# Attention scores from 16-bit parts of queries and keys, in a two-layer attention and FFN kernel

## The reference, cut to what matters

```python
q = (layernorm(x) @ Wq.T + bq)      # per head: [64, 8]
k = (ctx @ Wk.T + bk)
v = (ctx @ Wv.T + bv)
p = softmax(q @ k.T * sqrt(8))      # per sequence and head, [64, 64]
x = x + concat_heads(p @ v) @ Wp.T + bp
```

## Time and profile before

| | us |
|---|---|
| median of 3 runs (1026.54 to 1030.34) | 1029.37 |
| the profiled execution | 1027.88 |
| span of its profile | 1026.1 |
| PE busy | 872.3 (85%) |
| DVE busy | 775.2 (76%) |
| ACT busy | 581.3 (57%) |
| POOL busy | 567.8 (55%) |

### The profile page before, as it was taken

How to read it: one execution, slowest core, us unless ns; L and a number is a source line. 1 busy time by engine, 2 the same in 40 slices (tenths; PEclk the granted TensorE clock), 3 DMA queues, 4 the chain that set the end, 5 groups by cost and what they waited for, 6 DMA issues and landing times. The chain is left out here.

```text
span 1026.1 us, 25789 instructions
## 1 busy us (share of the span) xinstructions
PE 872.3 (85%) x9415; PEld 623.1 (61%) x9415; DVE 775.2 (76%) x2300; ACT 581.3 (57%) x940; POOL 567.8 (55%) x642
## 2 busy tenths in 40 slices
PE   6837999855878775999999537999999999979997
PEld 1215777633555444666666425888888888846665
DVE  6786999878878672988888555788898876547774
ACT  2464888543444342666667523576767656347774
POOL 4400476568777773555555476665656551027775
PEclk9967999889999997999999856999999999989999
DMA  8744555233223244444444221232424240023442
GB/s 252 257 145 114 158 169 152 80 126 112 73 73 83 73 134 126 120 156 158 153 151 153 79 78 33 70 90 89 136 79 124 62 116 12 23 84 81 131 117 52
DMA packets 86909, 114.74 MB, mean 112 GB/s; under 512 B 36384, under 2 KB 55520, under 8 KB 86016
## 3 DMA queue, kind: packets, MB, share of 16 engines
q1 hardware_dynamic: 75856, 94.99, 31.2%
q0 software_dynamic: 8192, 16.79, 5.6%
q10 hardware_dynamic: 2736, 1.31, 0.5%
HBM read 73.73 MB, written 35.13 MB: 106 GB/s over the span
## 5 line engine op out<-in xcount | busy, mean ns | idle before, releaser
L1128 POOL TENSOR_TENSOR moe_h_lo<-moe_hid,moe_h_hi 128x512 f16<-128x512 f32 x78 | 90.3, 1159 | 92.2 <-ACT moe_h_hi L1285 87.6
L1833 ACT ACTIVATE split_table<-attn_psT 128x1024 f32<-128x1024 f32 x64 | 65.3, 1021 | 95.1 <-PE attn_psT L1711 88.1
L1391 DVE SCALAR_TENSOR_TENSOR moe_hid<-moe_psU,split_to_hidden,moe_act_g 128x512 f32<-128x512 f32 x110 | 80.5, 745 | 24.2 <-ACT moe_act_g L1279 24.0
L1279 ACT ACTIVATE moe_act_g<-moe_psG,split_unscale 128x512 f32<-128x512 f32 x110 | 75.8, 689 | 40.5 <-PE moe_psU L1210 36.6
L1285 ACT ACTIVATE moe_h_hi<-moe_hid 128x512 f16<-128x512 f32 x110 | 68.6, 624 | 32.8 <-DVE moe_hid L1391 32.8
L1900 DVE TENSOR_REDUCE split_table<-attn_psN 128x16 f32<-128x1024 f32 x62 | 75.2, 1214 | 12.1 <-PE attn_psN L1686 12.0
L1122 POOL DMA_INDIRECT scratch_xs<-cell_xn,res_row x64 | 63.0, 985 | 25.6 <-issue 19.1
L1628 POOL DMA_INDIRECT cell_h<-scratch_ys,res_slot x64 | 62.7, 980 | 19.7 <-issue 19.7
L1122 POOL DMA_INDIRECT scratch_xs<-moe_xn,res_row x64 | 62.1, 970 | 19.5 <-issue 19.5
L1628 POOL DMA_INDIRECT cell_y<-scratch_ys,res_slot x64 | 62.5, 977 | 17.8 <-issue 17.4
L1723 PE MATMUL attn_psO<-heads_vheads,split_table 128*64 128x18 f32 x2048 | 71.4, 212 | 0.1
(11 more groups left out here) (353 smaller groups left out, 2776.9 us busy)
## 6 DMA issues: line engine op xcount, KB each, us to landing
early_ctxT<-in_keys SPq DMA_DIRECT2D x16, 512.0 KB, 3.6
scratch_ys<-cell_h SPq DMA_DIRECT2D x26, 256.0 KB, 2.0
early_ctxT<-in_values SPq DMA_DIRECT2D x8, 544.0 KB, 3.8
mlstm_vals<-in_values SPq DMA_DIRECT2D x8, 544.0 KB, 3.8
scratch_fw<-ffn_table SPq DMA_DIRECT2D x8, 544.0 KB, 4.7
res_x<-in_x SPq DMA_DIRECT2D x16, 256.0 KB, 6.1
early_ctxT<-in_ctxT SPq DMA_DIRECT2D x16, 256.0 KB, 6.1
attn_in_ctxT<-attn_in_ctxT SPq DMA_DIRECT2D x64, 64.0 KB
```

The costliest lines, as they stand in the source:

```text
L1128: pool.tensor_tensor(h_lo[u % 3][c][:, :], hid[u % 2][c][:, :], h_hi[u % 3][c][:, :], ALU.subtract).then_inc(lo_done[c], 1)
L1279: act.activation(act_g[c][:, :], psG[c][:, :], ACT.Silu, scale=sw.unscale[:, 0:1]).then_inc(silu_done, 1)
L1391: v.scalar_tensor_tensor(out=hid[u % 2][c][:, :], in0=psU[c][:, :], scalar=sw.to_hidden[:, 0:1], in1=act_g[c][:, :], op0=ALU.mult, op1=ALU ...
L1833: act.activation(probT[i % 2][:, :, :, :, :].rearrange("p r b m q -> p (r b m q)"), psT[:, :], ACT.Exp).then_inc(prob_done, 1)
```

## The change

In the experts' stage a new class `ScoreOperands` prepares the keys. `k_out` now adds the key bias. VectorE takes the largest absolute key of every group; in slot tiles 5 to 8 the three engines form from it, and from the query weights, two scales, and scale the query weights and bias in place. From slot tile 10 on ScalarE scales each group's keys and writes their f16 high part, GpSimd the f16 low part, and SP stores both in a scratch tensor `kh`; 32 such halves are spread over 29 slot tiles. In the attention phase the three key buffers are cleared once, and SP loads each group's keys into them by eight transfers of 16 rows each, which leaves the other places zero: this takes the place of `k_out`'s masks. To make that possible the columns of the query and key weights are permuted on the host.

The queries are written as a high part by ScalarE (`q_hi`), then VectorE computes the low part and writes both parts twice, with masks (`split_q`). The score products become three f16 products each: high times high, high times low, low times high. The scale is taken back in the exponential. From group 3 on the normalised rows are written by ScalarE (`normalise_more`) with a factor and a start value that GpSimd forms (`begin`). `q_(g+2)` moves ahead of `values(g, 0)` on TensorE, `hb.clear` moves behind the first normalise on VectorE.

```diff
+    def half(self, act, n, raw, pairs):
+        g = n // 2
+        keys, pair = raw[:, g * GROUP:(g + 1) * GROUP], pairs[g % 2]
+        if n % 2 == 0:
+            act.wait_ge(self.ready, ONE + 1)
+            act.activation(keys, keys, ACT.Copy, scale=self.all[:, 0:1]).then_inc(self.scaled, 1)
+        else:
+            act.wait_ge(self.scaled, ONE + g + 1)
+            if g >= 2:
+                act.wait_ge(self.kept, ONE + 16 * (g - 1))
+            act.activation(pair[:, 0, :], keys, ACT.Copy).then_inc(self.high_done, 1)
+    def low(self, pool, g, raw, pairs):
+        pair = pairs[g % 2]
+        pool.wait_ge(self.high_done, ONE + g + 1)
+        pool.tensor_tensor(pair[:, 1, :], raw[:, g * GROUP:(g + 1) * GROUP], pair[:, 0, :], ALU.subtract).then_inc(self.low_done, 1)
...
+            def load_keys(g):
+                if g >= 3:
+                    sp.wait_ge(scores_done, ONE + 4 * (g - 2))
+                else:
+                    sp.wait_ge(cleared, ONE + g + 1)
+                for rr in range(HR):
+                    for m in range(HM):
+                        rows = slice((rr * HM + m) * ROWS, (rr * HM + m + 1) * ROWS)
+                        sp.dma_start(keys[g % 3][rows, :, :, m, :].rearrange("p w b t -> p (w b) t"),
+                                     s["kh"][g, rows].rearrange("p w (b t) -> p (w b) t", b=GB)).then_inc(keys_in[g % 3], 16)
...
             for g in range(GROUPS):
+                if there(g + 3):
+                    load_keys(g + 3)
                 store(g)
...
+            def begin(g):
+                k = g % 2
+                pool.wait_ge(ln.var_done, ONE + g + 1)
...
+                pool.tensor_scalar(minus[k][:, :], ln.mv[k][:, :, 0], -1.0, None, ALU.mult).then_inc(minus_done, 1)
+                ln.root(pool, g, k)
...
+                pool.tensor_tensor(start[k][:, :], minus[k][:, :], ln.rstd[k][:, :], ALU.mult).then_inc(start_done, 1)
...
                 for b2 in range(2):
                     b = 2 * i + b2
-                    for rr in range(HR):
-                        rows = slice(rr * RH, (rr + 1) * RH)
-                        ins = pe.matmul(bank[:, rr * 512 + b2 * HM * S:rr * 512 + (b2 + 1) * HM * S],
-                                        queries[g % 3][rows, b, :, :].rearrange("p n t -> p (n t)"),
-                                        keys[g % 3][rows, b, :, :].rearrange("p m t -> p (m t)"), start=True, stop=True)
+                    for n, (wq_, wk_) in enumerate(((0, 0), (0, 1), (1, 0))):
+                        for rr in range(HR):
+                            rows = slice(rr * RH, (rr + 1) * RH)
+                            ins = pe.matmul(bank[:, rr * 512 + b2 * HM * S:rr * 512 + (b2 + 1) * HM * S],
+                                            queries[g % 3][rows, wq_, b, :, :].rearrange("p n t -> p (n t)"),
+                                            keys[g % 3][rows, wk_, b, :, :].rearrange("p m t -> p (m t)"),
+                                            start=(n == 0), stop=(n == 2))
...
+            def normalise_more(g):
+                act.wait_ge(x_turned, ONE + g)
+                act.wait_ge(start_done, ONE + g + 1 - ON_V)
+                for t in range(TILES):
+                    ins = act.activation(xn[:, t, :], res.x[:, g * TILES + t, :], ACT.Identity, bias=start[g % 2][:, t:t + 1],
+                                         scale=ln.rstd[g % 2][:, t:t + 1])
+                ins.then_inc(xn_more, 1)
...
+            def split_q(g):
+                pair = both[g % 2]
+                v.wait_ge(q_hi_done, ONE + g + 1)
+                v.scalar_tensor_tensor(out=pair[:, 1, :], in0=psF[:, :], scalar=bq[:, 0:1], in1=pair[:, 0, :],
+                                       op0=ALU.add, op1=ALU.subtract).then_inc(q_lo_done, 1)
+                v.wait_ge(q_lo_done, ONE + g + 1)
+                if g >= 3:
+                    v.wait_ge(scores_done, ONE + 4 * (g - 2))
+                for n in range(HN):
+                    ins = v.tensor_scalar(queries[g % 3][:, :, :, n, :].rearrange("p w b t -> p (w b) t"),
+                                          pair.rearrange("p w (b t) -> p (w b) t", b=GB), qmask[:, n:n + 1], None, ALU.mult)
+                ins.then_inc(q_done, 1)
...
                 if one:
                     peak_of(g + 1, 2)
+                if two:
+                    split_q(g + 2)
                 if now:
                     heads_out(g, 0)
...
-                if three:
-                    normalise(g + 3)
```

More of the change, by code:

```diff
@@ L303, in keep, with halves_at, keys_split_at, __init__ @@
         sp.dma_start(s["fw"][e], table[:, :]).then_inc(self.table_out, 16)
+K_TOP = 32768.0
+SPLIT_FROM = 10
+HALVES = 2 * GROUPS
+def halves_at(j):
+    if j < SPLIT_FROM:
+        return range(0)
+    n = SLOT_TILES - SPLIT_FROM
+    return range((j - SPLIT_FROM) * HALVES // n, (j - SPLIT_FROM + 1) * HALVES // n)
+def keys_split_at(j):
+    return [n // 2 for n in halves_at(j) if n % 2]
+class ScoreOperands:
+    def __init__(self, nc, ctx, sems, sw, given):
+        r = self.room = Room(nc, ctx, sems, "operands")
+        self.given, self.ident, self.ones = given, sw.ident, sw.ones
+        self.tops, self.wide, self.top = r.sb("tops", [P, GROUPS]), r.sb("wide", [P, 2]), r.sb("top", [P, 2])
+        self.one, self.scales, self.all = r.sb("one", [1, 2]), r.sb("scales", [1, 4]), r.sb("all", [P, 4])
+        self.unscore = r.sb("unscore", [P, 1])
+        self.read, self.step, self.fed, self.ready = r.sem("read"), r.sem("step"), r.sem("fed"), r.sem("ready")
+        self.scaled, self.high_done, self.low_done, self.kept = r.sem("scaled"), r.sem("high"), r.sem("low"), r.sem("kept")
+    def largest_key(self, v, g, raw, k_raw):
+        v.wait_ge(k_raw, ONE + g + 1)
+        v.tensor_reduce(self.tops[:, g:g + 1], raw[:, g * GROUP:(g + 1) * GROUP], AX.X, ALU.max,
+                        apply_absolute_value=True).then_inc(self.read, 1)
+    def largest(self, v):
+        step, given = Steps(v, self.step), self.given
+        v.wait_ge(given.loaded, ONE + 16 * given.count)
+        v.wait_ge(self.read, ONE + GROUPS)
+        v.tensor_reduce(self.top[:, 0:1], self.tops[:, :], AX.X, ALU.max)
+        v.tensor_reduce(self.wide[:, 0:1], given.wq[:, :], AX.X, ALU.max, apply_absolute_value=True)
+        step(v.tensor_reduce(self.wide[:, 1:2], given.bq[:, :], AX.X, ALU.max, apply_absolute_value=True))
+        step(v.tensor_reduce(self.top[:, 1:2], self.wide[:, :], AX.X, ALU.max))
+    def invert(self, v, ps):
+        step = Steps(v, self.step)
+        step.at(2)
+        v.wait_ge(self.fed, ONE + 1)
+        step(v.tensor_reduce(self.one[:, :], ps[0:1, 0:2 * P].rearrange("o (n p) -> o n p", n=2), AX.X, ALU.max))
+        step(v.tensor_scalar(self.scales[:, 2:4], self.one[:, :], TINY, 1.0 / K_TOP, ALU.max, ALU.mult))
+        step(v.reciprocal(self.scales[:, 0:2], self.scales[:, 2:4]))
+    def apply(self, v, ps):
+        step, given = Steps(v, self.step), self.given
+        step.at(5)
+        v.wait_ge(self.fed, ONE + 2)
+        step(v.tensor_copy(self.all[:, :], ps[:, 0:4]))
+        for t in (given.wq, given.bq):
+            v.tensor_scalar(t[:, :], t[:, :], self.all[:, 1:2], 0.5 / D, ALU.mult, ALU.mult)
+        v.scalar_tensor_tensor(out=self.unscore[:, :], in0=self.all[:, 2:3], scalar=2.0 * D * SCALE1, in1=self.all[:, 3:4],
+                               op0=ALU.mult, op1=ALU.mult).then_inc(self.ready, 1)
+    def turn_largest(self, pe, ps):
+        pe.wait_ge(self.step, ONE + 2)
+        for n in range(2):
+            ins = pe.matmul(ps[0:1, n * P:(n + 1) * P], self.top[:, n:n + 1], self.ident[:, :], start=True, stop=True)
+        ins.then_inc(self.fed, 1)
+    def spread(self, pe, ps):
+        pe.wait_ge(self.step, ONE + 5)
+        pe.matmul(ps[:, 0:4], self.ones[:, :], self.scales[:, :], start=True, stop=True).then_inc(self.fed, 1)
+    def half(self, act, n, raw, pairs):
[13 more added lines that the diff above has]
+        pool.tensor_tensor(pair[:, 1, :], raw[:, g * GROUP:(g + 1) * GROUP], pair[:, 0, :], ALU.subtract).then_inc(self.low_done, 1)
+    def keep(self, sp, s, g, pairs):
+        sp.wait_ge(self.low_done, ONE + g + 1)
+        if g:
+            sp.wait_ge(self.kept, ONE + 16 * g)
+        sp.dma_start(s["kh"][g], pairs[g % 2][:, :, :]).then_inc(self.kept, 16)
@@ L1006, in phase_moe @@
         xnT = [r.sb(f"xnT{k}", [D, GROUP]) for k in range(2)]
+        pairs = [xnT[k][:, :].bitcast(F16).rearrange("p (w t) -> p w t", w=2) for k in range(2)]
         x_hi = [r.sb(f"x_hi{k}", [D, GROUP], F16) for k in range(2)]
@@ L1111, in _ @@
                     fw.feed(sp, a, j // 2, piece)
+                if j + 1 < SLOT_TILES:
+                    for g in keys_split_at(j + 1):
+                        ops.keep(sp, s, g, pairs)
             for b in range(3):
                 sp.wait_ge(y_out[b], ONE + 16 * len(range(b, SLOT_TILES, 3)))
+            sp.wait_ge(ops.kept, ONE + 16 * GROUPS)
         @block.gpsimd
@@ L1140, in _ @@
```

(12 more changed lines are left out.)

159 lines of the change are left out of this document (95 added, 64 removed).

## The result

The changed kernel takes 1051.93 us (median, 1050.82 to 1054.44) against 1029.86 for the kernel before in the same comparison: a ratio of 1.022, interval 1.019 to 1.025. It is slower by 22 us, where 10 us less was forecast, with a range of 1002 to 1033. The profiled execution took 1051.22 us, its span is 1049.4, 23.3 more than before.

What follows compares the result with a forecast made beforehand. TensorE looked to bound the kernel; after the change the table loop would bind groups 2 to 8. Experts +0.5, start -0.7, table loop +4.7, end -14.5 sum to -10.0 us: forecast 1018, range 1002 to 1033.

Steps and rivals of the forecast that it cites:

- TensorE's term: Attention groups: scores steps fall from 1.37 to 0.89 us, plain from 0.97 to 0.66, saving 3.2 us of 17.53.
- VectorE's new work: Per attention group: split_q comes at 1.65 us (bounds 1.5 and 3.2), normalise's 2.96 goes, 1.3 us less work.
- the gather loop's landing: Attention gathers: 2.48 us from the fourth gather's start to VectorE's combine, one part of the gather loop.
- the prediction's own sum: Gather loop through GpSimd and VectorE: 15.5 us a group, or 16.9 with low, both under 17.53.
- the two small ops: GpSimd, between statistics and the last four gathers: two added ops, estimated at 0.45 us.
- SP's keys: Eight key transfers a group, 5 us of issue, behind the table's store and ahead of need: cost nothing.
- The table loop: Attention groups 2 to 8: the weight table's trip through memory becomes the bound, 18.2 against 17.53 us, +4.7 in all.
- The last seven intervals: End of attention: three intervals become 15.5 us each (-5.7), four follow TensorE (-8.8), together -14.5 us.
- The start: Start of attention: gathers already set the pace, so splitting earlier keys gains little, -0.7 us (+2 to -4).
- The experts' stage: Preparing keys on ScalarE, GpSimd and VectorE, partly in the router's stage, costs +0.5 us (0 to +4).
- The clock: Attention groups 2 to 8: TensorE, idle some 3 us a group, at times runs two steps at lower clock, +0.4.
- Rival (c): Slower: table loop lengthens to 20.5 us with split_q at 3.2 and half-clock steps; +12.5, 1040 us; chance 0.13.

Runs made afterwards that it cites:

- e1: Changed kernel with all eight gathers of group g+4 on GpSimd ahead of begin(g+3), not four before and four behind: 1025.33 us, ratio 0.996.
- e3: Changed kernel with the weight table's store and the raw weight load cut to 64 columns each in groups 1 to 8: 1036.7 us.
- e2: Changed kernel with each key load from group 3 on moving 2 of its 16 rows, same number of transfers: 1040.89 us.
- e10: Changed kernel with the cuts of e2 and e3 together, few key rows and small weight transfers: 1040.46 us.
- e8: Kernel before the change, with its gathers in e1's order and nothing else: 1024.38 us, ratio 0.994.
- e5: e1 with scores(g,3) put ahead of plain(g+2,0) on TensorE: 1020.95 us.
- e6: e1 with the weight table stored in two halves, the high half ahead of x3's store, and high waiting only for that half: 1020.89 us.
- e7: e1, e5 and e6 together, with the starting raw weight loads behind group 2's gathers and group 1's keys behind the second combine: 1008.8 us, ratio 0.979.
- e11: Changed kernel with VectorE's largest key taken over 16 of the 512 columns of each group: 1048.56 us.
- e12: e7 with three exchanges: shift before out_ and peak(g+2,0), plain(1+g,1) behind scores(g,0), values copied ahead of the fourth exponential: 1002.1 us, ratio 0.971.
- e4: Changed kernel with normalise back on VectorE for all groups and begin reduced to the square root: 1046.78 us.

## Why the prediction was wrong

**TensorE's term was nearly right.** Plain was forecast at 0.66 and is 0.66, scores at 0.89 and is 0.99: 2.8 us a group saved instead of 3.2. The missing 0.1 is the end of the step: from the last block's start to the values' matmuls 0.32 us pass (752.53 to 752.85), where the next block follows after 0.23. The first three of e1's intervals behind the store of group 8 are 14.66, 14.66 and 14.65, close to the 14.3 given for TensorE alone.

**VectorE's new work was right.** split_q 1.65 forecast, 1.57 measured; each f16 pass takes 469 to 562 ns in all 32, so no hold as long as the 2110 ns of the earlier trace rows came to them. GpSimd ran no arithmetic beside any of them, so the Trainium skill's rule on the shared port (SBUF — State Buffer, section Who interferes with whom) is not tested by this trace.

**The step that failed is the gather loop's landing.** The text took "a gather started at 634.92 let VectorE combine at 637.40, 2.48", from the start of the stage, where SP had no transfer under way, and carried it into groups 2 to 8. There the landing is 5.6. The rest of that sum stands: statistics to the fourth gather is 6.57 (6.19 forecast), and 16.9 + 0.38 + 3.15 = 20.4. e1 shows the place (the gathers out of the loop: -2.4 a group), e3 and e2 the reason (the weights 2.0, the keys 1.2), e10 that without both the landing is 2.6, near the 2.48 forecast.

The trace of the kernel before had it. The earlier trace rows end with the gather at 736.70, the fourth of its group; these lines are the combine that needed it, and the first of the four gathers:

```profile
742.28 1.14 DVE L1879 SCALAR_TENSOR_TENSOR res_x<-cell_y,res_cw,res_x 128x128 f32<-128x128 f32 x4 [0.85 <-DMA cell_y<-scratch_ys,res_slot]
```

```profile
732.79 1.10 POOL L1628 DMA_INDIRECT cell_y<-scratch_ys,res_slot  x1 [0.19 <-issue]
```

The combine came 5.58 us behind the fourth gather, and VectorE waited 0.85 us for it. In three of the eight turns from 665 to 805 us it waited so, 0.32 to 0.85, with landings of 5.05 to 5.58; in the other five it was late itself, and 4.64 to 4.87 only bounds the landing from above. With 5.58 in place of 2.48 the prediction's own sum is 20.0. Without split_q and the two small ops the same sum is 17.9, about the 17.53 of the kernel before: the gather loop was at that period already, with TensorE's work just under it (e8, with the gathers out of the loop, takes 16.98, and there TensorE is busy for 139.66 of 140 us). The change lengthened the loop by split_q (1.57) and by `begin` (0.82: 2.65 us against 732.79 - 730.96 = 1.83). So the mistake was to take a loop at its limit for one with room.

The collision is not chance: `out_`, which releases SP's transfers, and `begin`, which releases the last gathers, both stand close behind statistics (749.09 and 747.17 above), so they meet in every group, and the later the gathers end, the later both come in the next. In the kernel before they stand as close (`out_` at 733.07 in the earlier trace rows, the first of the four gathers at 732.79). How busy the DMA engines were between the fourth gather and the combine agrees, though not in proportion: the share is 0.19 for the landing that the prediction took, 0.62 and 0.90 for the two of over 5.5 us (columns as in the earlier trace rows, DMA share last but one; the first two lines are of the kernel before, the third of the changed one):

```profile
634.92:637.40 2.48, 2.48 (x26) 2.32 (x24) 0.00 (x0) 0.42 (x1) 2.45 (x3) 0.50 0.19 53
736.70:742.28 5.58, 5.04 (x82) 4.53 (x81) 4.66 (x9) 4.42 (x8) 4.79 (x5) 1.00 0.62 189
```

```profile
753.57:759.20 5.63, 3.58 (x62) 2.86 (x59) 0.55 (x3) 3.43 (x6) 4.83 (x5) 0.82 0.90 202
```

SP's keys were priced as issue time only ("nothing"); their traffic was not priced at all. That queues of different engines share the same DMA engines is also what the Trainium skill states (DMA: Bandwidth & Descriptors, section Issuing engines are not separate DMA queues: transfers "interleave with each other, regardless of the engine that started them"); the landings of 2.6, 3.1, 4.6 and 5.8 us agree.

**The table loop was real, and not the bound.** Forecast 18.2, it shows as soon as the gathers are gone: e5 has 17.85 with 15.8 us of waits for the table. Beside it lay a loop that the prediction did not have, S: split_q, low, statistics, peak, plain(g+2,0), scores(g,3), then 4.4 us of ScalarE's work before the next group's first exponential. It is as long (e6, 17.47). That these two are loops of one length is shown by e7, where both are opened and the intervals fall to 16.21; the parts of S were read from e1's waits.

**The last seven intervals** were to fall by 14.5 and fell by 3.1. Of the 11.4 us missing, 8.7 are in the first three (55.2 instead of 46.5), for the same reason, as the gathers go on to group 15 there; the interval of 21.45 us at group 10 follows the two weight loads that SP issues at 847.48. The other 2.7 are in the four behind them, which have no gathers; why is not shown. In e1 the seven fall by 12.8. The start was to gain 0.7 and lost 3.4: the second raw load, which the kernel before issued at 640.34, behind the masked keys, and the key loads now go out beside the first gathers (e7, with them later: 2.5 of it). The experts' stage, +0.5 forecast, +2.2 in this trace, stays open (e11).

**The clock.** Its fall to 0.89 follows the waits, and comes back to 1.00 in e12. That a loop which idles TensorE pays for the lower level each time, as the Trainium skill has it (TensorE: Matmul & The Clock Gate, section HAM oscillation), agrees with the scores step of 1.82 us at 0.50 behind a wait; what it adds to the period of 20.4 can't be told, since the sum of the gather loop holds no TensorE step.

Rival (c), slower, had the wrong loop: its price was 1040, and its condition, split_q at 3.2, did not come. Its sign, intervals over 19.5, did, by way of the gather loop. No rival had a gather landing over 2.48. Two of the prediction's sums are slightly off (5.74 + 0.45 + 2.48 is 8.67, and (c)'s three terms give 13.1), which changes nothing here.

## What to carry to other kernels

When a change makes the bounding engine faster, list every loop that passes through a transfer, and take the landing from the stretch in which it will run, with the traffic that will run beside it. Read it in the turns in which somebody did wait, however short the wait (0.3 to 0.9 us here); where nobody waits, the time to the consumer only bounds it from above. Look at which events release the transfers and the gathers: if one step releases both, they collide in every turn. Loops of equal length hide each other, so an exchange that seems to bring nothing alone may be half of one that does (e5 and e6 brought 4.4 us each on top of e1, and 16.5 together with the start).

## What the runs showed of the hardware

- Four gathers of 128 rows that land 2.6 us after the last one's start (e10) take 3.1 beside a group's key loads (2048 runs of 128 bytes, e3), 4.6 beside 1.1 MB of weights (e2), and 5.8 beside both (the changed kernel).
- Moving the gathers earlier against the same traffic did not make them land earlier by as much (e4: started 0.83 us earlier behind the statistics, landing 6.3 instead of 5.8).
- 16-bit pairs of 128 columns on the two halves of the rows take 0.06 us each in a step of 16 pairs at granted clock 1.00 (0.23 for four), and 0.1 at 0.50 behind a wait of 1.8 us (0.38 to 0.43 for four).
